# A second token sort in four stages, with pad stores moved between row loads, in a three-layer MoE kernel

## What is computed

```python
x = _layernorm(x + attn(x, Wq, Wk, Wv, Wo))            # 256 x 256 softmax scores per batch, shared by 16 heads
x = _layernorm(x + xattn(x, itok, ctx, ctx, ctx))      # expert chosen by token id: silu(x ctx.T) * (x ctx.T), then ctx.T
x = _layernorm(x + ffn(x, Wr, br, Wg, Wu, Wd))         # expert chosen by a router: top 1 of 4

# ffn, per token: e = argmax(softmax(x @ Wr + br)), weight = its probability
# out = weight * ((silu(x @ Wg[e]) * (x @ Wu[e])) @ Wd[e]),  Wg, Wu: 4 x 256 x 1024, Wd: 4 x 1024 x 256
```

## Time and profile before

| | |
|---|---|
| median of 3 executions | 184.02 us (183.65 to 184.31) |
| profiled execution | 184.34 us, of which the span from first to last instruction is 182.5 us |
| PE busy | 169.0 us, 93% of the span |
| POOL / DVE / ACT busy | 104.8 / 123.6 / 94.7 us |
| DMA | 35.28 MB, mean 193 GB/s |
| granted PE clock, mean | 0.985 of 2.4 GHz |

### The profile page before, as it was taken

How to read it: one execution, slowest core, us unless ns; L and a number is a source line. 1 busy time by engine, 2 the same in 40 slices (tenths; PEclk the granted TensorE clock), 3 DMA queues, 4 the chain that set the end, 5 groups by cost and what they waited for, 6 DMA issues and landing times.

```text
span 182.5 us, 3731 instructions
## 1 busy us (share of the span) xinstructions
PE 169.0 (93%) x947; PEld 125.6 (69%) x947; DVE 123.6 (68%) x400; ACT 94.7 (52%) x246; POOL 104.8 (57%) x126
## 2 busy tenths in 40 slices
PE   7999998899989999999999999999999999999910
PEld 2677776457867745778876788867888587867710
DVE  3389688878787777846554364444699966878780
ACT  2257979535565632438772466645566322445540
POOL 8100657544827565126997999943688700365563
PEclk9999999999999999999999999999999999999985
DMA  5999999337999523248867375653870004511101
GB/s 128 374 332 417 384 385 346 116 111 209 374 324 403 223 91 99 81 122 307 239 203 233 104 329 178 205 182 134 273 244 1 4 0 135 214 57 57 49 24 44
DMA packets 14404, 35.28 MB, mean 193 GB/s; under 512 B 1838, under 2 KB 8112, under 8 KB 14258
## 3 DMA queue, kind: packets, MB, share of 16 engines
q1 hardware_dynamic: 12752, 31.84, 50.6%
q0 software_dynamic: 1344, 3.22, 4.8%
q10 hardware_dynamic: 290, 0.01, 0.1%
HBM read 26.44 MB, written 8.88 MB: 194 GB/s over the span
## 4 chain that ended last, share of the span: by engine, by line
PE 52%; POOL 16%; DVE 12%; issue 10%; DMA 5%; ACT 2%; POOLq 2%; SPq 0%; DVEq 0%; ACTq 0%
PE bank L582 10%; PE bank L583 9%; PE bank L584 9%; POOL w_lo L490 7%; POOL out_tokens L571 4%; POOL rstd L494 3%; PE bank L888 3%; PE bank L780 3%; DMA x_sorted<-buf,slot 3%; PE bank L590 3%; PE bank L743 2%; DMA rows<-x_sorted 2%; PE bank L596 2%; PE bank L867 2%; PE bank L653 2%
## 5 line engine op out<-in xcount | busy, mean ns | idle before, releaser
L490 POOL TENSOR_TENSOR w_lo<-stage,w_hi 128x512 fp32r<-128x512 f32 x40 | 50.9, 1303 | 22.9 <-ACT w_hi L970 18.0
L1086 ACT ACTIVATE gate<-bank 128x256 f32<-128x256 f32 x40 | 15.4, 385 | 43.3 <-PE bank L584 37.9
L1487 DVE TENSOR_TENSOR hid<-bank,gate 128x256 f32<-128x256 f32 x40 | 17.0, 424 | 30.2 <-ACT gate L1086 30.0
L582 PE MATMUL bank<-w_hi,xr 128*128 x72 | 29.7, 412 | 0.7 <-POOL w_lo L490 0.4
L494 POOL TENSOR_TENSOR rstd<-mv,mhalf 128x1 f32<-128x1 f32 x16 | 9.7, 604 | 33.7 <-DVE mv L1233 33.4
L583 PE MATMUL bank<-w_lo,xr 128*128 x72 | 28.4, 394 | 0.0
L584 PE MATMUL bank<-w_hi,xr 128*128 x72 | 28.2, 392 | 0.0
L970 ACT ACTIVATE w_hi<-stage 128x512 fp32r<-128x512 f32 x45 | 26.9, 631 | 0.9 <-PE bank L584 0.9
L582 PE MATMUL bank<-w_hi,hT 128*128 x72 | 23.3, 324 | 0.1
L584 PE MATMUL bank<-w_hi,hT 128*128 x72 | 20.3, 282 | 0.0
L583 PE MATMUL bank<-w_lo,hT 128*128 x72 | 20.3, 282 | 0.0
(11 more groups left out here) (233 smaller groups left out, 342.5 us busy)
## 6 DMA issues: line engine op xcount, KB each, us to landing
stage<-in_w_ffn SPq DMA_DIRECT2D x15, 768.0 KB
arena<-in_w_ffn SPq DMA_DIRECT2D x8, 768.0 KB, 5.0
rows<-x_sorted SPq DMA_DIRECT2D x19, 132.0 KB, 2.2
x_sorted<-xr SPq DMA_DIRECT2D x2, 1056.0 KB, 6.2
x_sorted<-xr SPq DMA_DIRECT2D x1, 1584.0 KB
buf<-in_x_tok SPq DMA_DIRECT2D x1, 1024.0 KB, 11.3
w_hi<-in_ctx SPq DMA_DIRECT2D x1, 1024.0 KB
w_hi<-in_ctxT SPq DMA_DIRECT2D x1, 1024.0 KB, 14.1
```

Of the source, the lines that this page charges most:

```text
L490: g.tensor_tensor(out=lo, in0=src, in1=hi.bitcast(F32), op=ALU.subtract).then_inc(split_lo, 1)
L582: mm(dst, xhi, whi, start=start, stop=False)
L1086: a(gate[:, (T + j) % 2, :], fA[j % 2][:, 0:FQ], ACT.Silu).then_inc(silu_done, 1)
L1487: v.tensor_tensor(out=hid[:, (T + j) % 2, :], in0=fA[j % 2][:, FQ:2 * FQ], in1=gate[:, (T + j) % 2, :], op=ALU.mult).then_inc(h_done, 1)
```

## The change

The second sort is cut into four stages instead of two. Blocks 0 and 1 are chosen from the counts of tiles 0 to 4, block 2 from tiles 0 to 6, block 3 from tiles 0 to 7, the rest from all. Two pad stores of 1056 KB move from behind the loads of all ten sorted tiles to between those of tile 2 and tile 3. PE no longer reads weight offsets from a table, but works them out in registers from the row number of the block. The shared block's weights are loaded one half before block 8's rows, one half behind its own rows. The pieces of the weights are split in another order, and in quarter 0 all of them beside items 4 to 9. Three sums are copied by ACT instead of DVE, and PE's, ACT's and DVE's programs for the first five items are written out.

```diff
-ROUTED = 7
+ROUTED = [5, 7, 8, T]
             for t in range(EARLY):
                 sorted_rows(t)
+            load_pads(1)
+            load_pads(2)
             sp.wait_ge(d_scat1[1], 16 * (CHUNKS - 2 * SORTED))
             sp.wait_ge(tables, 1)
             for t in range(EARLY, T):
...
-            for i in range(1, len(PAD_PARTS)):
-                load_pads(i)
+            load_pads(3)
...
+            r0 = first_row(0)
+            sp.wait_ge(d_scat2[0], 16 * ROUTED[0])
+            routed_row(0, r0)
+            routed_row(1, first_row(1))
             sp.wait_ge(row_table, 2)
...
+            sp.wait_ge(row_table, 5)
+            for t in range(LATE, LATE + 2):
+                routed_row(t, first_row(t))
...
+            joint_row = [first_row(JOINT)]
+            joint = [expert_at(joint_row[0]) * P]
+            load_half(0, 0)
+            for t in range(LATE + 2, JOINT):
+                routed_row(t, first_row(t))
+            joint_rows(0)
+            joint_row.append(first_row(JOINT + 1))
+            joint.append(expert_at(joint_row[1]) * P)
+            joint_rows(1)
+            load_half(0, 1)
...
-        share = [[0, 0, 1, 1, 2, 2, 2, 2, 2, 0], [1, 1, 2, 1, 2, 1, 2, 1, 1, 0], [1, 1, 2, 1, 2, 1, 2, 1, 1, 0]]
+        UP_FIRST = [(0, 0), (0, 1), (0, 2), (1, 0), (1, 1), (2, 0), (2, 1), (1, 2), (3, 0), (3, 1), (2, 2), (3, 2)]
+        share = [[0, 0, 0, 0, 2, 2, 2, 2, 2, 2], [1, 1, 2, 1, 2, 1, 2, 1, 1, 0], [1, 1, 2, 1, 2, 1, 2, 1, 1, 0]]
...
-                    pe.wait_ge(split_lo, (q + 1) * Q_PIECES - len(LO_BY_DVE))
+                    pe.wait_ge(split_lo, q * Q_PIECES + (UP_PIECES if q else Q_PIECES) - len(LO_BY_DVE))
...
-            idle_products(20)
-            rank(3)
-            idle_products(6)
+            idle_products(14)
...
+            w_off(0)
             ftx(0)
+            idle_products(3)
+            rank(3)
+            ftx(1)
+            fup(0)
+            ftx(2)
+            fup(1)
+            fth(0)
+            fup(2)
...
+            first_chosen()
+            penalties()
+            next_row(2, T + 2, GROUP_OF[ROUTED[1] - 1])
             shifts(3)
             choose(3)
+            fxlo(0)
             place(3)
```

More of the change, by code:

```diff
@@ L275, in route_kernel, with expert_at @@
         LOS_BEFORE, LOS_BEHIND = 4, [2, 2]
+        def expert_at(row):
+            return nc.s_assert_within((row * 31 + 3200) >> 15, 0, E - 1,
+                                      skip_runtime_bounds_check_because="at most (4096 * 31 + 3200) >> 15, which is 3")
+        assert all((b * P * 31 + 3200) >> 15 == min(b // CHUNKS, E - 1) for b in range(BLOCKS2))
         def wait_los_of(eng, n):
-            k = (n + 1) * PIECES
             if n < E:
@@ L421, in _, with joint_rows @@
[L421 to L424, removed]
+                    load_half(q, h)
+            def joint_rows(h):
+                sp.dma_start(rows[h * SMALL:(h + 1) * SMALL, JOINT, :],
+                             scr2[bass.ds(joint_row[h], SMALL), :]).then_inc(d_rows[JOINT], 16)
@@ L553, in _ @@
             pool.wait_ge(d_init2[3], 32)
-            for t in range(ROUTED, T):
+            for t in range(GROUPS[3][0], T):
                 scatter2(t)
@@ L904, in fdown @@
                 last.then_inc(y_done, 1)
-            pe.wait_ge(tables, 2)
+            w_off(0)
             ftx(0)
-            for i in range(len(items) + 2):
-                if i == EARLY:
-                    fth(i - 1)
[L911 to L929, removed]
+            idle_products(3)
[6 more added lines that the diff above has]
+            fup(2)
+            fth(1)
+            fdown(0)
+            ftx(3)
+            fth(2)
+            fdown(1)
+            fup(3)
+            ftx(4)
+            fdown(2)
+            fth(3)
+            ftx(5)
+            fup(4)
+            for i in range(5, len(items) + 2):
+                if 5 < i and i + 1 < JOINT:
+                    ftx(i + 1)
+                if i < len(items):
+                    fup(i)
+                if i == 5 or i + 1 == JOINT:
+                    ftx(i + 1)
+                if i <= len(items):
+                    fth(i - 1)
+                fdown(i - 2)
         @block.scalar
@@ new lines, in next_row @@
+            def next_row(t, row, group):
+                c = t - FIRST2
+                whole_of(row, group)
+                step(v.scalar_tensor_tensor(out=next_key[:], in0=whole[:], scalar=-2.0 * BLOCKS, in1=penalty[:],
+                                            op0=ALU.mult, op1=ALU.add))
+                step(v.tensor_reduce(out=next_of[:, c:c + 1], in_=next_key[:], axis=AX.X, op=ALU.min))
+                v.tensor_scalar(out=row2[:, t:t + 1], in0=next_of[:, c:c + 1], scalar1=2.0 * BLOCKS, scalar2=float(P),
+                                op0=ALU.add, op1=ALU.mult).then_inc(row_table, 1)
@@ L1404, in late_rows @@
[L1404 to L1413 removed]
+                step(v.tensor_tensor(out=by_size[:, 0, :], in0=whole[:], in1=chosen[:], op=ALU.subtract))
```

278 lines of the change are left out of this document (161 added, 117 removed).

## The result

The changed kernel takes 189.37 us (median of 5 executions, 188.45 to 190.91), the kernel before 184.01 (183.44 to 184.31) beside it: a ratio of 1.0306, 95% interval 1.0277 to 1.0335. It is 3% slower. The forecast was 183.6 us, in a range up to 185.3: wrong in its sign and outside its range. The profiled execution of the changed kernel took 190.91 us, the slowest of the five and 1.5 us above the median, so a time read from its trace can be late by as much.

The account below looks back on a forecast made before the run. The prediction took PE, 93% busy, as the bound, with only waits before and inside quarter 0 to win. Its terms, +1.9 and -2.3, gave -0.4 us: 183.6 us from a median of 184.02, range 181.6 to 185.3.

Parts of the forecast that it names:

- What bounds the kernel: Only PE's waits before and inside quarter 0 can be won; any delay of PE in stage B is lost in full.
- X: PE's first `fup` of quarter 1, at 97.83 before; forecast at 95.5, with the end moving as it moves.
- Term 1: Stage B's start: tile 3's load queues behind the moved pad stores, +1.9 us, bounds 0 to 2.7.
- Terms 2 and 3: Quarter 0's earlier start and what its tail gives back: together quarter 1 starts 2.3 us earlier, bounds 1.0 to 2.9.
- Term 2: Start of quarter 0: early blocks let the first `fup` start at 69.15, 2.5 us before 71.65.
- Term 3: Tail of quarter 0: later row numbers, 0.8 to 1.0 us wait for block 8, chunk 7 landing at 92.2.
- (b): Tail of quarter 0: row numbers 1 us later delay block 8, second half and chunk 7; 184.9 to 185.5 us, chance 0.21.
- (a): Stage B's start: tile 3's load isn't held by the stores; 181.7 us, up to 182.4, chance 0.24.
- (c): Stage B: PE's wait before tile 3 lowers its clock, costing some 2 us; 185.6 us, chance 0.04.
- (d): Quarter 0: early blocks buy nothing, PE waits for block 2 or 3 as long as gained; 185.5 us, chance 0.05.

Follow-up runs that it names:

- e5: Changed kernel with one pad store instead of two between the loads of tiles 2 and 3, the other back behind the ten loads: 185.58 us, ratio 1.0120.
- e2: Changed kernel with all pad stores back behind the ten tile loads, as in the kernel before: 183.53 us, ratio 0.9986.
- e3: Changed kernel with both pad stores issued behind SP's wait for the last scatter, just ahead of tile 3's load: 191.42 us, ratio 1.0399.
- e1: Kernel before with only the two pad stores moved between the loads of tiles 2 and 3: 189.80 us, ratio 1.0312.
- e10: Changed kernel with the two pad stores issued in POOL's queue, right behind stage A's last scatter: 190.93 us, ratio 1.0349.
- e9: Second profile of the kernel before, unchanged: the profiled execution took 184.40 us.
- e6: e2 with the first half of the shared block's weights behind block 8's rows instead of ahead of them: 183.18 us, ratio 0.9975.
- e7: e6 with chunk 7 also ahead of the second half of the shared block's weights: 184.47 us, ratio 1.0037.
- e12: e2 with the kernel before's split order of the pieces and chunk 7 issued between the two shared weight halves: 183.85 us, ratio 1.0001.

## Why the prediction was wrong, point by point

**What bounds the kernel** held. Stage B has no slack, and what delays tile 3 is lost: in e5 PE takes it 1.7 us later than in e2 (43.84, 42.15), and the time is 2.05 us longer. The distance from X to the end was 84.9 us in the changed kernel (189.1 - 104.24), 84.7 in the forecast; over the eleven profiles of versions with the four stages most are longer, 85.0 to 85.8 in eight of them.

**Term 1 failed.** The step is the sentence that the last scatter of stage A "isn't stuck behind the stores, only slowed", and with it the issue of tile 3's load at 40.3. The scatter was stuck: 7.56 us against 2.91, no packet for 3 us. The load's queueing behind the stores, on which Term 1 spent its working, is real (7.26 us in e3), but happens there and not in the changed kernel. The estimate of when the pair of stores lands was a little short: 7.8 us after the first issue against 8.7 (37.54 to 46.2). What was missing is that the scatter lands with the stores, at 45.46, that the load is issued only then, and that it needs its own 2.2 us on top. The term measured +5.8 us where +1.9 was written, of which 4.6 are the scatter and most of the rest the clock (0.9 to 1.5). The upper bound of 2.7 was no bound: it let the scatter be "slowed" by a tenth of the rate, and no row showed a scatter of POOL behind a store of SP. The shared rows of 66 KB that needed 4.8 us behind two weight halves are of one queue, but the case that the scatter fares as they do deserved a bound of its own. In sequence, 43.9 for the stores plus 2.2 for the load would have given 46.1, 3.7 us late instead of 1.9, and 185.4 by the rest of the sum: still short of 189.4. The stores went out 1.4 us later than the prediction has them in this profiled execution (37.54, not 36.1; 36.09 in e1), the clock comes on top, and Terms 2 and 3 gave less.

The Trainium skill, page "DMA: Bandwidth & Descriptors", section "Queues, rings and completion order", says that an engine takes turns between queues packet by packet; the measurement differs, 0 packets of the waiting queue in 3 us against 578 and 275 of the other one (changed kernel and e10), and the measurement decides. The same section says that a completion is written only after every earlier write of that engine, across its queues. The forecast didn't weigh that a completion can be late by stores of another queue; the packets of q0 show that here the data came late as well.

**Terms 2 and 3** had the moves right and gave them too much. With the pads back (e2) the first `ftx` ran at 67.03 (forecast 67.2), the first `fup` at 68.73 (69.15) and X at 95.69 (95.5), which looks like a hit. It is in part luck: in that execution stage B ended 0.6 us earlier than in the trace that the forecast counts from (63.43, 64.04), and it was the second fastest of its ten. Counted from the idle products behind stage B, and over all eleven profiles of versions with the four stages:

| from the end of stage B to | kernel before, e9, e1 | forecast | four stages, 11 profiles |
|---|---|---|---|
| first `fup` | 7.6 to 7.9 us | 5.1 | 5.2 to 6.2 |
| last row numbers | 12.6 to 12.9 | 15.3 | 15.7 to 16.8 |

PE's wait for block 0's rows, for which Term 2 has 0.1 us, is 0.4 to 1.4 us in each of the eleven. Term 2 takes 2.44 us for tile 4's scatter and 2.11 for the load behind it; they were 2.82 and 2.03 in e2, 3.29 and 2.53 in the changed kernel. The last row numbers, which release blocks 6 to 8 and with them the half, the shared rows and chunk 7, come 0.4 to 1.5 us later than Term 3 has them. With the 0.5 us lost behind X that makes Terms 2 and 3 together worth 1.1 to 1.2 us by two profiles of each kernel and 0.26 us by the medians (no change within the interval), not 2.3. And each order of the three large transfers at the end of quarter 0 gave what it gained to another wait of PE (e6, e7, e12). No trace was taken of an execution at the median of both kernels, so the last 0.9 us are known from times alone. A slip in Term 2's sum changes little: three `fup`, one `fdown` and five transposes at its own rates are 5.96 us, not 5.6.

In the changed kernel itself nothing of the gain was left at X: from the end of stage B to X it is 34.4 us (69.85 to 104.24), in the kernel before 33.8, in e2 32.3. PE waited 1.24 us for block 0, 0.93 for block 8 and 1.53 for the pieces. Chunk 7 was issued at 93.56 and needed 7.14 us, against 86.7 + 5.5. The last row numbers came 5.1 us behind the ones before them, in DVE's timeline:

```profile
81.12 0.16 DVE L1440 SCALAR_TENSOR_TENSOR row<-block_no,ones_f 128x2 int32<-128x2 f32 x1
...
86.25 0.16 DVE L1440 SCALAR_TENSOR_TENSOR row<-block_no,ones_f 128x5 int32<-128x5 f32 x1
```

That is 16.6 us behind the end of stage B, 1.3 more than Term 3 has, and the mechanism of rival (b). Whether the moved pads have a part in chunk 7's 7.14 us isn't shown: e3 and e10, with the pads moved too, have 34.0 and 33.6 us from the end of stage B to X.

**Rivals.** (a), a load that isn't held, is out: e3 and e10. (b) is true in its mechanism, as said, and not what decides: e2 has that tail and is not slower. (c) came true and had a chance of 0.04, because it was weighed for a wait of 1.9 us; the wait was 3.8. It cost 0.9 to 1.5 us, 2 was written. e5, with a wait of 1.65 us and a clock of 1.00, is the case that the prediction reasoned about, and there it was right. (d) is out as it was put, since the early blocks did bring the start of quarter 0 forward by 1.4 to 2.7 us, but its sign was there: PE waited 1.24 us for block 0's rows, at 74.28. No rival had the case that happened, a scatter that a store in another queue holds, and that is why the range ended 4 us short.

## What to carry to other kernels

A large store didn't cost only what stood behind it in its own queue: in these runs a small transfer that something waited for had to be ahead of it in time, in either queue, or wait for nearly all of it. Before a store is moved into a gap, list every transfer still to be issued from there on, in all queues, and add their waits in series: here the scatter, then the load that waits for it. And when a wait of PE grows longer than any that the traces show without a fall of the clock, price PE's slower start with it. A gain that is read from one profile of each kernel should be set against how that point scatters between two profiles of the same kernel.

## What the runs showed of the hardware

- 132 KB issued behind 2.1 MB of stores landed after 7.0 to 7.6 us in the same queue and across queues, SP's behind POOL's and POOL's behind SP's, 2.0 to 2.9 us without them. Neither of the two queues was a way around. Behind one store of 1056 KB it was 5.05 us.
- The granted clock stayed at 1.00 behind a wait of PE of 1.65 us, and was 0.53 in the 3.4 us behind one of 3.8 us; a wait of 3.2 us brought products of 1.69 us instead of 0.88. Idle products ahead of the wait held it at 1.00.
- One point of the trace, X, differs by 1.1 us between two executions of one kernel (95.69 and 96.78).
